# A transformer block with three attentions on one core: eight more matmul sites follow the tiling that TensorE is in

## The reference

```python
x = attention(ln32(x, ln1), ln32(x, ln1), Wq1, Wkv1, Wo1, bo1) + x   # 16 heads of 16, 1024 keys
x = attention(ln32(x, ln2), context, Wq2, Wkv2, Wo2, bo2) + x        # 16 heads of 16, 154 keys
h = ln32(x, ln3) @ Wff1 + bff1                                       # 2 * 1024 wide
lin, gate = split(h)
x = (lin * gate * sigmoid(1.702 * gate)) @ Wff2 + bff2 + x
q, k, v = x @ Wq.T + bq, context @ Wk.T + bk, context @ Wv.T + bv    # one head of 256
out = softmax(q @ k.T) @ v + x
```

## Time and profile before

| | |
|---|---|
| median of 3 runs | 1566.27 us (1561.78 to 1571.61) |
| the profiled execution | 1567.2 us, span 1565.4 us |
| TensorE matmuls, weight loads | 17882 and 17882 |
| mean granted TensorE clock | 0.985 of full speed |
| VectorE, ScalarE, GpSimd busy | 71%, 60%, 16% |

### The profile page before, as it was taken

The page is one execution under the profiler, slowest core; times in us unless marked ns, Lnnn a source line. Parts: engine busy times, 40 slices in busy tenths (PEclk is TensorE's granted clock), DMA queues, the critical chain, the costliest instruction groups (busy, mean ns, idle before and its releaser), DMA issues.

```text
span 1565.4 us, 43994 instructions
## 1 busy us (share of the span) xinstructions
PE 1506.3 (96%) x17882; PEld 1016.7 (65%) x17882; DVE 1104.9 (71%) x2269; ACT 945.8 (60%) x1928; POOL 251.5 (16%) x347
## 2 busy tenths in 40 slices
PE   6899999999999999999999999999999999997887
PEld 5555555675767667676766767566666657574676
DVE  4577797858687686958778696867778686943443
ACT  4366776656666565666756576675656565664343
POOL 2210322111212012121211112201001110101110
PEclk9899999999999999999999999999999999998899
DMA  8824464446341431646142252446332251413210
GB/s 230 192 72 116 133 116 106 97 103 118 85 96 55 105 92 53 132 99 131 53 105 73 75 101 76 116 73 125 66 79 62 60 101 41 106 47 77 59 36 14
DMA packets 228863, 143.89 MB, mean 92 GB/s; under 512 B 92787, under 2 KB 220597, under 8 KB 228405
## 3 DMA queue, kind: packets, MB, share of 16 engines
q1 hardware_dynamic: 228597, 141.07, 38.4%
q10 hardware_dynamic: 64, 0.02, 0.0%
HBM read 92.68 MB, written 47.74 MB: 90 GB/s over the span
## 4 chain that ended last, share of the span: by engine, by line
PE 81%; DVE 9%; ACT 3%; DMA 2%; issue 2%; SPq 2%; POOL 0%; DVEq 0%; POOLq 0%; ACTq 0%
PE ps_o L1807 13%; PE ps_last L1716 11%; PE ps_last L1726 7%; PE ps_max L1443 6%; PE ps_s L1443 6%; PE ps_s L1440 6%; PE ps_max L1440 6%; DVE mxh L1400 5%; PE ps_pre L1553 4%; PE ps_pre L1562 3%; PE ps_last L1562 2%; PE ps_cross L1654 2%; PE ps_cross L1658 2%; PE ps_last L1757 2%; PE ps_cross L1632 1%
## 5 line engine op out<-in xcount | busy, mean ns | idle before, releaser
L1400 DVE TENSOR_REDUCE mxh<-ps_max 128x1 f32<-128x512 f32 x1024 | 656.2, 683 | 123.1 <-PE ps_max L1443 83.5
L1183 ACT ACTIVATE probs<-ps_s 128x512 f32<-128x512 f32 x1024 | 573.7, 599 | 213.7 <-PE ps_s L1443 113.8
L1807 PE MATMUL ps_o<-probs,vg 128*17 128x256 f32 x4096 | 290.8, 381 | 0.2 <-ACT o_sb L1189 0.2
L1440 PE MATMUL ps_s<-qst,kst 98*32 98x256 bf16 x4280 | 190.5, 272 | 0.8 <-ACT probs L1183 0.2
L1440 PE MATMUL ps_max<-kst,qst 96*32 96x512 bf16 x2052 | 187.0, 382 | 4.3 <-DVE mxh L1400 1.4
L1358 DVE SCALAR_TENSOR_TENSOR th<-th,gb 128x256 f32<-128x256 f32 x128 | 59.2, 463 | 160.7 <-ACT gb L1158 160.3
L1443 PE MATMUL ps_max<-kst,qst 96*128 96x512 bf16 x511 | 165.7, 383 | 5.7 <-DVE mxh L1400 4.2
L1443 PE MATMUL ps_s<-qst,kst 98*128 98x256 bf16 x978 | 167.1, 273 | 1.5 <-ACT probs L1183 0.5
L1440 PEld LDWEIGHTS ps_s<-qst,kst 98*32 98x32 bf16 x4280 | 112.8, 96 | 74.8 <-ACT probs L1183 15.9
L1807 PEld LDWEIGHTS ps_o<-probs,vg 128*17 128x17 f32 x4096 | 99.6, 97 | 83.4 <-issue 32.3
L1716 PE MATMUL ps_last<-y_hi,wff_hi 128*128 128x256 f32 x448 | 139.8, 312 | 4.1 <-DVE hT L1361 2.4
(11 more groups left out here) (278 smaller groups left out, 2115.4 us busy)
## 6 DMA issues: line engine op xcount, KB each, us to landing
vg<-v_s SPq DMA_DIRECT2D x64, 272.0 KB, 3.9
parts_s<-qk_parts SPq DMA_DIRECT2D x28, 384.0 KB, 3.9
o_s<-o_sb SPq DMA_DIRECT2D x64, 128.0 KB, 2.5
o_s<-o_sb SPq DMA_DIRECT2D x32, 256.0 KB, 2.2
oT<-o_s SPq DMA_DIRECT2D x62, 128.0 KB
den<-o_s SPq DMA_DIRECT2D x62, 128.0 KB
q_s<-qk_parts SPq DMA_DIRECT2D x16, 384.0 KB, 2.7
q2st<-q_s SPq DMA_DIRECT2D x16, 384.0 KB, 5.4
```

The costliest lines, as they stand in the source:

```text
L1183: nc.scalar.activation(probs[:, step % PR, 2 * pair:2 * pair + 2, :].rearrange("p j q -> p (j q)"), ps_s[pair][:, :], ACT.Exp, scale=SCALE ...
L1400: nc.vector.tensor_reduce(mxh[:, i % PAIRS, i // PAIRS:i // PAIRS + 1], ps_max[i % 2][:, :], AX_X, ALU.max).then_inc(g_mx, 1)
L1440: last = mm(bank[j * W:(j + 1) * W, cols_], keys[:, j * W:(j + 1) * W], queries, start=True, stop=True, tile_position=(0, j * W))
L1807: last = mm(ps_o[j * W:j * W + VW, 0:CH], vg[:, unit % VSLOTS, kt, j * VW:(j + 1) * VW], probs[:, step % PR, j, :], start=(kt == 0), stop= ...
```

## The change

`score`'s choice is moved into a new function `product`, which also passes `start` and `stop`. `project`, `project_rows`, the cross maxima, FF2 and both matmuls of the last attention now go through it and no longer call `whole()`. The two turns of maxima go through `few_turned`: with the array in columns, one narrow matmul by the identity takes the place of the transpose. The turns of lines 1544 and 1749, FF1 and the setup still call `whole()`. The table `ORDERS` is the same. Line numbers after the change are up to ten higher.

```diff
-            def score(bank, cols_, keys, queries):
+            def product(bank, cols_, weights, moving, start, stop):
                 if array["columns"]:
                     for j in range(G):
-                        last = mm(bank[j * W:(j + 1) * W, cols_], keys[:, j * W:(j + 1) * W], queries,
-                                  start=True, stop=True, tile_position=(0, j * W))
+                        last = mm(bank[j * W:(j + 1) * W, cols_], weights[:, j * W:(j + 1) * W], moving,
+                                  start=start, stop=stop, tile_position=(0, j * W))
                 else:
-                    last = mm(bank[:, cols_], keys, queries, start=True, stop=True)
+                    last = mm(bank[:, cols_], weights, moving, start=start, stop=stop)
                 return last
+            def score(bank, cols_, keys, queries):
+                return product(bank, cols_, keys, queries, True, True)
+            def few_turned(bank, rows, x):
+                if array["columns"]:
+                    return mm(bank[0:rows, 0:P], x, ident[:, :], start=True, stop=True, tile_position=(0, 0))
+                return nc.tensor.transpose(bank[0:rows, 0:P], x, ident[:, :])
...
             def project(bank, w, y):
-                whole()
                 for m in range(KD):
                     for k in range(KD):
-                        last = mm(bank[:, m * CH:(m + 1) * CH], w[:, k, m * P:(m + 1) * P], y[:, k, :],
-                                  start=(k == 0), stop=(k == KD - 1))
+                        last = product(bank, slice(m * CH, (m + 1) * CH), w[:, k, m * P:(m + 1) * P], y[:, k, :],
+                                       k == 0, k == KD - 1)
...
-                        whole()
                         for j in range(nh):
-                            last = mm(cross_max_banks[spare][f % 2][:, j * CTX:(j + 1) * CTX], q2st[0:ROWS, h0 + j, i * P:(i + 1) * P],
-                                      k2st[0:ROWS, h0 + j, 0:CTX], start=True, stop=True)
+                            last = score(cross_max_banks[spare][f % 2], slice(j * CTX, (j + 1) * CTX),
+                                         q2st[0:ROWS, h0 + j, i * P:(i + 1) * P], k2st[0:ROWS, h0 + j, 0:CTX])
...
                     for m in range((q % 2) * FM // 2, (q % 2 + 1) * FM // 2):
-                        last = mm(bank_[:, i * D:(i + 1) * D], hTs[e][:, m, i * P:(i + 1) * P], wff2[:, m, :],
-                                  start=(m == 0), stop=(m == FM - 1))
+                        last = product(bank_, slice(i * D, (i + 1) * D), hTs[e][:, m, i * P:(i + 1) * P], wff2[:, m, :],
+                                       m == 0, m == FM - 1)
...
             def max_turn(unit):
                 pe.wait_ge(g_mp, unit + 1)
-                whole()
-                nc.tensor.transpose(ps_max[0][0:PAIRS, 0:P], mxq[:, :], ident[:, :]).then_inc(g_mT, 1)
+                few_turned(ps_max[0], PAIRS, mxq[:, :]).then_inc(g_mT, 1)
```

More of the change, by code:

```diff
@@ L1548, in project @@
             def project(bank, w, y):
-                whole()
                 for m in range(KD):
                     for k in range(KD):
-                        last = mm(bank[:, m * CH:(m + 1) * CH], w[:, k, m * P:(m + 1) * P], y[:, k, :],
-                                  start=(k == 0), stop=(k == KD - 1))
+                        last = product(bank, slice(m * CH, (m + 1) * CH), w[:, k, m * P:(m + 1) * P], y[:, k, :],
+                                       k == 0, k == KD - 1)
                 return last
             def project_rows(bank, y, w):
-                whole()
                 for i in range(TT):
                     for k in range(KD):
-                        last = mm(bank[:, i * D:(i + 1) * D], y[:, k, i * P:(i + 1) * P], w[:, k, :],
-                                  start=(k == 0), stop=(k == KD - 1))
+                        last = product(bank, slice(i * D, (i + 1) * D), y[:, k, i * P:(i + 1) * P], w[:, k, :],
+                                       k == 0, k == KD - 1)
                 return last
@@ L1636, in cross @@
                     pe.wait_ge(c_mx, (o + 1) * 2 * Q2F)
-                    whole()
-                    nc.tensor.transpose(ps_cross[0:H * TT, 0:P], mx2[:, :, :].rearrange("p h i -> p (h i)"),
-                                        ident[:, :]).then_inc(c_mT, 1)
+                    few_turned(ps_cross, H * TT, mx2[:, :, :].rearrange("p h i -> p (h i)")).then_inc(c_mT, 1)
                     for _ in range(3):
@@ L1736, in last @@
                 pe.wait_ge(c_tab, (o // CPB + 1) * 48)
-                whole()
                 for i in range(TT):
                     for k in range(KD):
-                        last = mm(bank_[:, i * CH:i * CH + CTX], den2s[e][:, k, i * P:(i + 1) * P], m3[:, k, :],
-                                  start=(k == 0), stop=(k == KD - 1))
+                        last = product(bank_, slice(i * CH, i * CH + CTX), den2s[e][:, k, i * P:(i + 1) * P], m3[:, k, :],
+                                       k == 0, k == KD - 1)
                 last.then_inc(c_s3, 1)
@@ L1753, in last @@
                 pe.wait_ge(c_pTc, o + 1)
-                whole()
                 for i in range(TT):
                     for a in range(2):
-                        last = mm(bank_[:, i * D:(i + 1) * D], p3Ts[late][:, a, i * P:(i + 1) * P], vp[:, a, :],
-                                  start=(a == 0), stop=(a == 1))
+                        last = product(bank_, slice(i * D, (i + 1) * D), p3Ts[late][:, a, i * P:(i + 1) * P], vp[:, a, :],
+                                       a == 0, a == 1)
                 last.then_inc(c_av3, 1)
```

## The result

The change takes 1578.61 us (median of 8 runs, 1575.01 to 1580.92) where the kernel before took 1569.11 beside it. The ratio is 1.0064, 95% interval 1.0050 to 1.0078: 9.5 us slower. 1558 us were forecast, and the range ended at 1578. The profiled execution took 1575.4 us, span 1573.6, 8.2 us over the span of before.

A forecast was written before the change was run, and what follows sets the result against it. The kernel was taken as bound by TensorE, but not everywhere. -7.7 - 8.5 + 0.8 + 5.4 = -10.0 us of TensorE's time, times 0.83, gave -8.3 us and 1558 us; range 1546 to 1578.

The forecast's parts named there:

- parts 1 to 3 and 5: Array passages into columns -7.7 us, back to whole -8.5; open weight loads +0.8; narrow f32 and score groups cost nothing more.
- part 6: 467 cross maxima as groups of four narrow matmuls: 0 to 19.6 us more, taken as 0.
- The first rival: Narrow cross-maxima groups take 0.108 us for 0.066, 19.6 us more, 16.3 on the path: 1574 us; chance 0.20.
- Part 4: 49 of 80 turns of maxima become f32 matmuls of two passes, 0.11 us a pass: 5.4 us more.
- 0.83: Share of TensorE's saving that reaches the end: 81% of the chain on TensorE plus 2% issue.
- passages are hidden anyway: Passages lie mostly where TensorE next waits for a maximum, so the saving becomes longer waits: 1566 us; chance 0.12.
- the 2% of "issue": Chain time waiting for nothing shown, 31 us, about two thirds of what 454 passages cost; argued against hidden passages.

The follow-up runs named there:

- the run with the turns alone: Only the turns of maxima become matmuls inside narrow stretches, against the kernel before: ratio 1.0017.
- 148-passage table: All the change's sites, but each group's form comes from a run-length table counting narrow groups as free; ratio to the kernel before 0.9972, 1564.38 us.
- the NoOps: Kernel before with 12006 workless NoOps added on TensorE: 1947.98 us with them behind the whole groups, 1998.88 us in front.
- both engines are cut: VectorE's maxima and ScalarE's exponentials both cut short: kernel before 1534.14 us, change 1533.40, table counting 15 ns per narrow group 1524.61.

## Why the prediction was wrong

Right, by its own steps: parts 1 to 3 and 5 (TensorE's passages fell by 17 us start to start, groups of f32 work cost 0.43 us narrow as whole); part 6 (0.067 us, median of 292 steps, for 0.066). The first rival gave the right side for a reason that the trace refutes. Part 4 is neither shown nor refuted at the end of the program: the run with the turns alone has 30 of them as matmuls and 11 passages fewer each way, +1.0 us by the forecast's prices for these, +3.9 by its expectation, which counts that a passage is often only moved, and +2.6 was measured (0.3 to 5.0). On TensorE itself part 4 seems too dear: 42 of the change's 49 stand between narrow pieces, and the next piece starts 12 ns (median) after the turn does, where part 4 took 0.22 us.

Wrong is the sentence "No wait and no transfer is added, and no instruction passes another, so only TensorE's durations change", and with it "What comes of it in the end is what lies on the chain", 0.83. TensorE's own time came out, though scores do pass the second half of a narrow turn (rows at 225 us below); that the waits stay as they are did not. Three things failed.

1. The 0.83 was the share of a chain that the change itself shifts. TensorE has a semaphore of VectorE or ScalarE before it at nearly every maximum and every pair of scores, and an earlier TensorE waits there; its loads wait 9.0 and 3.2 us longer at the first attention's. In the 148-passage table 32 us less in passages, 22.9 us of TensorE's time by the prices of before's rows, became 5.8 us of time. The rival "passages are hidden anyway" (1566 us, chance 0.12) named this; its counter-argument, the 2% of "issue", counts passages, not what follows a wait further on.
2. A narrow group is handed over 25 ns later. I had priced a group by what it costs TensorE from start to start, not by when its last result can be read. The change makes 229 maxima and 524 scores newly narrow, and 467 cross maxima. Shown is the 25 ns. Cutting VectorE's reductions takes some 7 us of the loss away, with some 6 us of uncertainty. That the later results are what makes the kernel slower than before is argued and not shown, as no run changes them alone, and longer waits for transfers are a rival for a few us; how much of VectorE's +15.4 is this handover and how much is the gain lost in waits was not separated.
3. More instructions come with pauses of 0.1 to 3.3 us, 3.0 us in the change's own trace. I had looked for a limit on issue in each group and found none; these came four times in 47358 loads and matmuls.

How the pauses arise was not tested by itself, as the NoOps cost time of their own. The Trainium skill, Runtime: NRT & Kernel Launch, section Instruction fetch mechanics, says that instructions come in blocks of 16 KiB, 256 instructions, over a DMA queue of the sequencer's own, and that crossing a block is mostly hidden. The traces agree on the block: the change's 47358 loads and matmuls, with 338 instructions of TensorE's sequencer, are 186 times 256, and q8 has 186 packets for 3.05 MB. They agree with "mostly" too: four of the 186 come with a pause, of 0.5 to 1.0 us. Which crossings pause no run here shows. The DMA engines' share in the 2 us before a pause has a median of 0.54 over all 64 pauses of the traces without NoOps, where it is 0.2 to 0.3 at a packet in general, but some pauses came at 0.1.

Why the parts don't add up (turns on top of the rest cost more than alone) stays open; so does which transfer sets the pace when both engines are cut.

## What to carry over

A saving on the busiest engine is worth its price only up to the next wait; where it meets other engines more than once a microsecond, ask at each wait what that engine does with the time, and don't multiply by the chain's share. A cheaper form of an instruction has two prices, when the next can start and when its result can be read, and the second is paid by whoever waits. Put passages and narrow work where nobody waits (no run here tried that by itself), and count instructions: with a form that takes eight for two the pauses of an engine that waits for nothing grew from 0 to 3.0 us here.

## What was not expected of the hardware

- Four narrow loads and matmuls of 154 columns pass in 67 ns, eight instructions, group after group; NoOps on the same queue start 71 ns apart, one by one.
- The narrow turn of maxima takes one quarter of the array, and matmuls in the other quarters don't wait for it. Timeline of the change at 225 us:

```profile
225.12 0.28 PE L1453 MATMUL ps_max<-ident,mxq 128*8 128x128 f32 x1
225.13 0.29 PE L1440 MATMUL ps_s<-qst,kst 98*32 98x256 bf16 x3
225.24 0.27 PE L1453 MATMUL ps_max<-ident,mxq 128*8 128x128 f32 x1
225.25 0.37 PE L1440 MATMUL ps_s<-qst,kst 98*32 98x256 bf16 x4
```

Three of the four scores of the next group start 10 ns after the turn's first pass, beside it.

- Pauses with no wait of up to 3.3 us on TensorE, some at recurring instructions, that end between 1.15 and 2.1 us after a 16 KiB packet of the instruction queue; that window is part of how they are counted here. The first in the change's trace, in the middle of one group of values:

```profile
209.98 0.60 PE L1808 MATMUL ps_o<-probs,vg 128*17 128x256 f32 x6
211.58 0.39 PE L1808 MATMUL ps_o<-probs,vg 128*17 128x256 f32 x1 [0.99 <-issue]
```

```profile
210.00:211.50 1.50, 0.59 (x10) 0.09 (x3) 0.90 (x2) 0.48 (x1) 0.00 (x0) 1.00 1.16 135
```

The DMA engines' share in that stretch is 1.16. It is 1.17 in the same stretch of before, where TensorE doesn't pause, so busy DMA alone doesn't do it.
